# Row fills in halves beside sets two to five, and spare bf16 matmuls where TensorE waits

## Time and profile before

| | us |
|---|---|
| median of three runs | 497.14 |
| lowest, highest | 496.58, 505.9 |
| the profiled execution's own time | 495.54 |
| its span, first to last instruction | 493.8 |
| PE, DVE, ACT, POOL busy in the span | 447.9, 386.2, 321.9, 234.2 |

### The profile page before, as it was taken

One profiled execution on the slowest core, in us unless ns is written; L12 is line 12 of the kernel. 1 busy time (PEld: TensorE's weight loads), 2 busy tenths in 40 slices (PEclk: granted clock), 3 DMA queues, 4 the chain that ended last, 5 costly groups with the idle time before them and its releaser, 6 DMA issues.

```text
span 493.8 us, 17187 instructions
## 1 busy us (share of the span) xinstructions
PE 447.9 (91%) x6720; PEld 302.8 (61%) x6720; DVE 386.2 (78%) x1099; ACT 321.9 (65%) x660; POOL 234.2 (47%) x290
## 2 busy tenths in 40 slices
PE   3478989899999998899999999999999999999981
PEld 2365656556666665577767666666666666666761
DVE  6587897778878878889988877888889987877552
ACT  2345765457676667678777676667677787777841
POOL 6246576856734534454554444334444543222345
PEclk9657998899999999999999999999999999999997
DMA  7644343643433444433433322222244341220001
GB/s 125 167 101 104 91 102 82 142 115 87 106 84 93 111 110 98 101 93 94 91 77 62 68 51 68 68 69 69 53 86 94 76 93 47 63 56 14 14 23 32
DMA packets 71579, 40.48 MB, mean 82 GB/s; under 512 B 7896, under 2 KB 70584, under 8 KB 71500
## 3 DMA queue, kind: packets, MB, share of 16 engines
q1 hardware_dynamic: 69280, 36.04, 30.2%
q0 software_dynamic: 2112, 3.24, 4.7%
q10 hardware_dynamic: 108, 0.10, 0.1%
HBM read 4.74 MB, written 1.05 MB: 12 GB/s over the span
## 4 chain that ended last, share of the span: by engine, by line
PE 76%; DVE 10%; DMA 4%; issue 3%; ACT 2%; POOL 2%; SPq 1%; POOLq 0%; DVEq 0%; ACTq 0%
PE attn_ps L1016 17%; PE o_ps L1043 15%; PE misc_ps L1073 6%; PE misc_ps L1064 5%; PE misc_ps L978 5%; PE misc_ps L1050 4%; PE score_ps L897 4%; PE misc_ps L984 3%; PE misc_ps L979 3%; DVE max_words L823 3%; PE misc_ps L1056 2%; DVE normed_in L759 2%; PE misc_ps L995 2%; DMA c_tok<-in_ctx_dram 2%; PE score_ps L930 2%
## 5 line engine op out<-in xcount | busy, mean ns | idle before, releaser
L823 DVE TENSOR_REDUCE max_words<-score_ps 128x4 f32<-128x512 f32 x288 | 193.7, 683 | 50.5 <-PE score_ps L930 47.6
L703 ACT ACTIVATE probs<-attn_ps 128x512 f32<-128x512 f32 x288 | 169.7, 601 | 74.4 <-PE attn_ps L1016 68.5
L1016 PE MATMUL attn_ps<-pairs 55*128 55x128 bf16 (+1 forms) x1152 | 113.7, 220 | 9.0 <-DMA pairs<-max_rows 3.4
L930 PE MATMUL score_ps<-pairs 52*128 52x128 bf16 (+1 forms) x1152 | 115.4, 222 | 2.3 <-DMA pairs<-terms 2.0
L560 POOL TENSOR_TENSOR rest<-qk_f,terms 128x512 f32<-128x512 f32 x38 | 44.2, 1162 | 114.2 <-ACT terms L654 114.2
L1016 PEld LDWEIGHTS attn_ps<-pairs 55*128 55x128 bf16 (+1 forms) x1152 | 64.9, 95 | 53.3 <-issue 26.8
L1043 PE MATMUL o_ps<-probs,v 128*32 128x128 f32 x2304 | 96.8, 281 | 0.1
L930 PEld LDWEIGHTS score_ps<-pairs 52*128 52x128 bf16 (+1 forms) x1152 | 67.3, 96 | 6.5 <-DMA pairs<-terms 2.8
L1043 PEld LDWEIGHTS o_ps<-probs,v 128*32 128x32 f32 x2304 | 53.5, 109 | 23.4 <-issue 9.5
L568 POOL TENSOR_TENSOR terms<-rest,terms 128x512 bf16<-128x512 f32 x38 | 44.0, 1158 | 9.7 <-DVE max_words L836 7.2
L712 ACT ACTIVATE o_sb<-o_ps 128x256 f32<-128x256 f32 x80 | 30.9, 386 | 23.7 <-PE o_ps L1043 22.7
(11 more groups left out here) (121 smaller groups left out, 751.0 us busy)
## 6 DMA issues: line engine op xcount, KB each, us to landing
pairs<-terms SPq DMA_DIRECT2D x240, 128.0 KB
x_tok<-in_x_dram SPq DMA_DIRECT2D x8, 128.0 KB, 2.6
c_tok<-in_ctx_dram SPq DMA_DIRECT2D x8, 128.0 KB, 3.0
pairs<-max_rows SPq DMA_DIRECT2D x64, 12.0 KB
w<-in_weights_dram POOLq DMA_DIRECT2D x8, 128.0 KB, 3.2
out_dram<-x_tok SPq DMA_DIRECT2D x8, 128.0 KB, 1.8
w<-in_weights_dram POOLq DMA_DIRECT2D x5, 192.0 KB, 3.3
pairs<-template POOLq DMA_DIRECT2D x4, 112.0 KB, 7.9
```

The lines of the kernel that those rows point to most:

```text
L703: act.activation(probs[n % PROBS_RING][:, :, :].rearrange("p h q -> p (h q)"), attn_ps[n % 2][:, :], ACT.Exp, scale=float(D // HEADS[part] ...
L823: dve.tensor_reduce(max_words[ub(step) % 2][:, QUAD * g:QUAD * (g + 1)], score_ps[n % 2][:, :].rearrange("p (h k) -> p h k", h=QUAD), AX_X ...
L930: return pe.matmul(score_ps[NUM[step] % 2][:, j * S:(j + 1) * S], tile[score_rows(u), QUAD * g + j, 0, b * S:(b + 1) * S], tile[score_rows ...
L1016: last = pe.matmul(attn_ps[n % 2][:, j * S:(j + 1) * S], pairs[attn_rows(u), h, 1, b * S:(b + 1) * S], pairs[attn_rows(u), h, 0, b * S:(b ...
```

## The change

The four row fills are cut in halves of eight heads (56 KB) and moved: POOL issues the first half of fill r behind its own `rest` of unit r + 2, the second behind `term2` of that unit. Each fill has a semaphore of its own, and `mask_rows` of unit 8 + r waits for that one alone (32 counts for two halves). SP's wait at unit 8 is dropped. New is `spare(bank, n)`: n bf16 matmuls of the identity with itself into 128 columns of the bank that the step is about to write; the real work overwrites them. They stand behind the wait for the bank and ahead of the wait for the step's input. How many is a table, by kind of step and by min(unit, 3), in L0 alone. The two waits in `attn` change places.

```diff
+SPARE_AT = {"raw_tr": (16, 8, 0, 0), "ln_tr": (30, 16, 8, 0), "qk": (14, 14, 8, 0), "n_tr": (8, 0, 0, 0),
+            "a_tr": (6, 6, 6, 6), "attn": (16, 8, 6, 6)}
...
-        fill16_landed = sem("fill16_landed")
+        fill16_landed = [sem(f"fill16_landed{r}") for r in range(RING)]
...
-        def fill_rows(pool, r):
+        def fill_rows(pool, r, heads):
...
-            pool.dma_start(pairs16[r // 2][rows_, :, :, :].rearrange("p h a n -> p h (a n)"),
+            pool.dma_start(pairs16[r // 2][rows_, heads, :, :].rearrange("p h a n -> p h (a n)"),
                            template[first:first + MASK_ROWS + TERMS, :, :, :].rearrange("p a b n -> p (a b n)")
-                           .unsqueeze(1).to_broadcast([MASK_ROWS + TERMS, 16, 2 * TOK])).then_inc(fill16_landed, 16)
+                           .unsqueeze(1).to_broadcast([MASK_ROWS + TERMS, 8, 2 * TOK])).then_inc(fill16_landed[r], 16)
...
-                        if u == SETS:
-                            sp.wait_ge(fill16_landed, 16 * RING)
...
             pool.wait_ge(rows_ready, 3)
-            fill_rows(pool, 0)
-            fill_rows(pool, 1)
...
-                    pool.wait_ge(fill16_landed, 16 * RING)
+                    pool.wait_ge(fill16_landed[u], 32)
...
                 if step.kind == "ln_in" and u == 0:
-                    fill_rows(pool, 2)
-                    fill_rows(pool, 3)
...
+                if step.kind in ("rest", "term2") and SPLIT_BY_DVE <= u < SPLIT_BY_DVE + RING:
+
+                    if u == SPLIT_BY_DVE:
+                        pool.wait_ge(rows_ready, 3)
+                    fill_rows(pool, u - SPLIT_BY_DVE, slice(0, 8) if step.kind == "rest" else slice(8, 16))
...
+            def spare(bank, n):
+
+
+                for _ in range(n):
+                    pe.matmul(bank[:, 0:P], ident_bf[:, :], ident_bf[:, :], start=True, stop=True, skip_group_check=True)
...
+                if kind in MISC and kind in SPARE_AT:
+                    spare(bank, SPARE_AT[kind][min(u, 3)] if part == L0 else 0)
...
+                    if n >= 2:
+
+                        pe.wait_ge(exp_done, n - 1)
+                    if g == 0 and part == L0:
+                        spare(attn_ps[n % 2], SPARE_AT["attn"][min(u, 3)])
                     if g == 0:
 
                         pe.wait_ge(max_landed[m % 4], (m // 4 + 1) * 16)
-                    if n >= 2:
-
-                        pe.wait_ge(exp_done, n - 1)
```

## The result

The change was forecast at 494.1 us and 0.6% faster. It is slower by a little: the median of its 20 runs is 502.54 us (497.17 to 510.11), that of the kernel before, run beside it, 502.19 us (494.38 to 508.95). The ratio of the compared runs is 1.0082, with a 95% interval from 1.0047 to 1.0117. The sign was wrong. The profiled execution took 500.74 us against 495.54, so 5.2 us have to be found between the two traces.

The account below looks back on a forecast made before the run. PE's own work was taken to set the pace behind 120 us, so early gains stay; -4.5 (tokens) + 0.3 (fills) - 2.2 (clock) + 3.4 (spares) = -3.0 us gave 494.1 us, range 488.8 to 499.5.

Parts of the forecast that it names:

- What bounds the kernel: Whole kernel: PE's own work sets the pace behind 120 us, so what the beginning gains or loses stays one to one.
- the rivals: Four other outcomes: 489.8 us (chance 0.22), 497.2 us (0.15), 501.9 us (0.08) and 497.1 us (0.05).
- The rival that was slower: L0: all 120 later spares cost, +6.8, and fills' halves hold up maxima, +2.5; with the tokens +4.8, 501.9 us; chance 0.08.
- Tokens of set 1, -4.5: Setup: without four fills DVE starts set 1 at 10.76 instead of 15.26 us, -4.5 us, kept at 3 to 5.5.
- Fills, +0.3: Units 2 to 5: eight half fills cost POOL issue time and may delay maxima, 0 to 2.5 us, taken as +0.3.
- q0 would have no share before 30 us: Sign in the DMA view: POOL's queue, which carried the fills, shows no share before 30 us.
- The clock, -2.2: Four stretches up to 79 us: spares keep the clock full in about half; -4.3 us if everywhere, -2.2 taken.
- spares on the path, +3.4: Units 2 to 7: spares not covered by PE's waits, 1.0 us in units 2 and 3, 2.4 in 4 to 7; bounds 1.5 to 6.8.

Follow-up runs that it names:

- after_guard_again: The whole change with the guard, run a second time: 495.23 us, ratio 0.9979 to the kernel before.
- after_guard: The whole change with the guard: 494.09 us, ratio 0.9962 to the kernel before.
- ntr8_spares: The changed kernel with 36 more spares ahead of the `n_tr` of unit 8, second half: 503.24 us.
- fills_only: The changed kernel with all counts of spares set to nothing, the fills moved: 507.01 us, ratio 1.023 to the kernel before.
- spares_only: The changed kernel's spares, with the fills whole in the setup as before: 502.71 us, ratio 1.0161 to the kernel before.
- after_again: The changed kernel run a second time, without the guard: 499.74 us, ratio 1.0068 to the kernel before.
- ntr9_spares: The changed kernel with 36 more spares ahead of one `n_tr` of unit 9, a unit past the wait meant: 502.59 us, ratio 1.0113 to the kernel before.
- no_atr6: The changed kernel without the six spares at `a_tr` of unit 6: 495.8 us.
- setup_spares: The changed kernel without the spares at `a_tr` and `attn` from unit 2 on: 503.55 us.
- setup_guard: The changed kernel without the spares at `a_tr` and `attn` from unit 2 on, with the guard: 499.41 us, ratio 1.0046 to the kernel before.
- the guard: An added wait: POOL's `rest` of units 10 to 15 waits for DVE's first maximum of the unit two before; on the changed kernel 494.09 us.
- guard8: The change with the guard, and `rest` of unit 8 waiting for the maximum of unit 6: 495.75 us, ratio 0.9954 to the kernel before.
- ntr_spares: The changed kernel with eight more spares ahead of every `n_tr` of units 6 to 11: 503.77 us, ratio 1.0166 to the kernel before.
- half_guard: The change with the guard and three late spares in place of six: 498.86 us, ratio 1.0017 to the kernel before.
- before_guard: The kernel before with the guard and no part of the change: 499.95 us, ratio 1.0072 to the kernel before.
- before_late: The kernel before with ten matmuls of the identity ahead of the last scores of unit 8: 502.74 us.
- before_again: The kernel before, run once more for another trace: 495.48 us, one run.

## Why the prediction was wrong

**What bounds the kernel: the step that failed.** "What the beginning gains or loses stays in the sum one to one, and nothing can be gained behind it." I had taken the stretch behind 100 us as one in which PE's work alone sets the pace, because PE is busy there all the time. It was busy because DVE's small operations won a race with POOL by 0.20 us, a margin in no view of busy time. My sum priced spares only by PE's time, on the path or beside it, and asked nowhere which two engines a delay of 0.33 us would put in another order. None of the rivals had it. The rival that was slower had the right sign by the wrong mechanism: late spares at full price (+6.8) and held-up fills (+2.5). Unit 8 started ahead of before all the same, where that rival had it behind. (The rival also counts 120 later spares. There are 108 at `a_tr` and `attn` in units 2 to 7, 6.2 us at 57 ns, and 16 more in unit 2's preparation.)

**The loss in numbers.** Units 8 to 10 take 26.7 us after and 19.8 before: 6.9 us. PE's wait explains 1.8 of them (2.16 in place of 0.38), and the rest, 5.1 us, goes with 10.2 us at 1.2 GHz, some 0.5 a microsecond. Where operations were held up and the low stretch was 3.4 us, the distance is 24.0 in both traces; with none held up and none low it is 19.8 to 20.8 in seven executions of six kernels. A fall alone (after_guard_again, 13.7 us) makes it 26.2, 5.4 us more than after_guard's, 0.39 a microsecond. So the clock costs an estimated 0.4 to 0.5 us a microsecond here. That share is argued from distances of different executions; no run changed the clock alone. That the wait brings the fall is argued too, from six traces out of six (last section); ntr8_spares was to test it and couldn't.

**Tokens of set 1, -4.5: right.** DVE's statistics start at 10.83 us against the forecast 10.76, straight behind the constants of 10.59, and the first unit gains 5.6 us, at the upper bound of 5.5. In fills_only, which has no spares, it gains 4.6 (25.9 in place of 30.5), so about 1 us of the 5.6 goes with the spares of the setup. The timeline after:

```profile
10.59 0.15 DVE L751 TENSOR_SCALAR half_m<-col 128x4 f32<-128x4 f32 x1
...
10.83 0.28 DVE L741 BATCH_NORM_STATS2 stats<-x_tok 128x6 f32<-128x128 f32 x1
```

**Fills, +0.3: right in size, by another way.** An issue takes 0.61 us at the median and a half lands in 3.2, so neither POOL nor the engines are held. What they do cost lies at DVE. An issue now stands between two of POOL's operations, and DVE's normalization beside them is stretched more than in the earlier trace rows (chain of waits after, which answers to its 1.11 and 2.81):

```profile
26.45 3.53 DVE normed_in L760 x4
...
36.17 3.48 DVE normed_in L760 x4
```

That is 0.7 us twice, in fills_only too (3.53 and 3.48), while spares_only, with the fills in the setup, has 2.81 both times. The prediction had said that q0 would have no share before 30 us; the first half is issued at 27.50. Units 2 and 5 still start 5.1 and 4.9 us ahead of before.

**The clock, -2.2, and spares on the path, +3.4: the sum fits, neither size is known.** By unit 8 the forecast is -3.0 and the profiled execution has -3.3. But how far one trace can be trusted is seen in seven executions whose kernels don't differ up to there (after, after_again, after_guard, after_guard_again, ntr9_spares, ntr8_spares, no_atr6): they place it at 96.3 to 99.5 us, at 97.9 in the mean, which is 1.2 to 4.4 us ahead of the kernel before (100.7 and 100.8). So a gain of that size is real, but the nearness to -3.0 is in part luck. Without the late spares unit 8 comes at 96.2 and 96.0 (setup_spares, setup_guard), on average 1.8 us ahead of those seven, and spares_only is 0.3 behind the kernel before; both are less than 3.4, but they are net of what the clock gave back, and no run parts the two. The clock did answer, though not where I looked. From 17 to 41 us it was low for 24 us before and for 7 after. Where it shows in the time is units 6 to 10: with the guard, late spares make the difference between 499.41 (setup_guard, whose trace has 20.5 us at the low clock there) and 494.09 us (after_guard, none there).

**The forecast itself** was that of a kernel in which the order holds: after_guard, 494.09 and 495.23 us, ratio 0.9962 [0.9938, 0.9987]. That is 1.9 us less than before where -3.0 was forecast, so that the first of these medians equals the forecast 494.1 is luck. In its first group it is distinct from no change. The repetition's interval reaches over 1 (0.9979 [0.9906, 1.0053]). With guard8 (0.9954 [0.9905, 1.0004]) it is the best version here.

**What stays open.** It isn't known what decides whether the clock falls behind a wait of medium length (below), nor what holding the clock through the wait of 2.16 us would give back. A lighter guard, on the maximum just before, wasn't tried.

## What to carry to other kernels

Before adding even 0.3 us to one engine, list in the trace the small DVE operations with two SBUF inputs that a critical engine waits for, and how far ahead of POOL's long operations they start: a margin under the added time is a risk of several microseconds, and it shows in no busy share. Where the order matters, say it with a semaphore instead of leaving it to the timing; here one wait on an engine with slack was worth 4.5 us of the changed kernel's median on the same chip. It is no gain by itself, though: with it the kernel before, in whose two traces the order holds anyway, was 0.7% slower. And follow a gain by marks through the whole kernel: the change was 3.3 us ahead at unit 8, and only marks show that it was lost behind that. One trace a kernel is not enough for the small terms: the mark at unit 8 moved by 3.2 us between executions of kernels that are alike up to there.

## What the runs showed of the hardware

- A 128x16 DVE operation of 0.17 us took 0.92 to 1.08 us when a POOL operation of 1.15 us had started 0.13 to 0.27 us before it, and its successor another 1.07 to 1.08: two operations were held up by two, since DVE's second waited for the first and came behind POOL's second.
- PE idle for 1.52 to 2.16 us at that step was followed by the low clock in all six traces that had it at the high clock (after, after_again, ntr9_spares, spares_only, ntr_spares, setup_spares), from 1.2 to 2.1 us behind the wait's end, for 3.4 to 10.2 us. Waits of 0.39 and 0.53 us at the step (no_atr6, half_guard) were not. In another place a wait of that length doesn't decide it: PE's wait for the stack of maxima near 198 to 215 us was followed by the low clock within 2 us in after (1.57 us), after_again (1.49), spares_only (1.55) and after_guard (1.21), and by none in before (1.51), before_guard (1.46), ntr9_spares (1.71) and ntr_spares (1.78).
- Waits of 0.7 to 1.1 us for the stack of maxima, near 95 to 100 us, are not alike: the clock fell within 3 us of 0.94 us in after_guard_again and of 0.97 in before_late, and not behind these two of before_again:

```profile
95.74 0.40 PE L1016 MATMUL attn_ps<-pairs 99*128 99x128 bf16 x4 [0.97 <-DMA pairs<-max_rows]
...
99.90 0.40 PE L1016 MATMUL attn_ps<-pairs 99*128 99x128 bf16 x4 [0.78 <-DMA pairs<-max_rows]
```

- Once it has fallen the clock can stay low for as much as 20 to 27 us though PE is nearly full (fills_only: 8.52 of 10 us busy at 0.50 from 110 to 120 us) or full (setup_guard: busy all through from 98 to 118 us at 0.50).
